# Pair slots of a vision tower on one core: values' products in another bank, the rank a slot later, the second norm's scale behind the transposes

## The chip, the cores and the metric

The kernel runs on one core of one Trainium2 chip. The metric is the device time of one execution in microseconds (us). The engines named below are TensorE (PE in the rows, its weight loads PEld), VectorE (DVE), ScalarE (ACT), GpSimd (POOL) and SyncE (SP, which issues DMAs). The engines run their own instruction streams in order and meet only at semaphores.

## The reference

Three stages follow each other: a patch tokenizer, windowed attention at several pooling levels, and a transformer block with a mixture of experts. The change lies in the third:

```python
def _L0_ffn_ref(x, norm1_w, norm1_b, qkv_w, ...):
    xn = _layernorm(x, norm1_w, norm1_b)                    # 64 images, 49 tokens, 192 features, 12 heads
    qkv = (xn @ qkv_w.T + qkv_b).reshape(Bx, Nx, 3, H, hd).transpose(2, 0, 3, 1, 4)
    attn = softmax(einsum('bhqd,bhkd->bhqk', q, k) * scale)
    o = einsum('bhqk,bhkd->bqhd', attn, v)
    x = x + (o @ proj_w.T + proj_b)
    xn2 = _layernorm(x, norm2_w, norm2_b)                   # the second norm
    logits = xn2 @ w_gate                                   # 8 experts, the best 2 of each token
    gates = softmax(top_vals)
    moe_out = sum over experts of gate * (gelu(xn2 @ W1 + b1) @ W2 + b2)
    return x + moe_out
```

## The kernel before, in words

The tokenizer and the windowed attention take the first 490 us and are not touched. Then come 39 **pair slots** (490 to 840 us). Two images make a pair (`NP` = 32 pairs, 98 tokens on 128 partitions). `run_slots` runs one function per engine, `slot(item)`, and `item(lag)` is the pair that entered `lag` slots ago, so each slot works on eight pairs at different steps, n0 (just entered) to n7. Slots 0 to 7 fill the pipeline, slots 8 to 31 are full (a hardware loop of two slots a turn), slots 32 to 38 empty it. Slots 7 to 31 have all of n0 to n7.

What each engine does in a full slot is the order in which its `slot` is written out:

- GpSimd (`gpsimd`, from L499): for n0 the **root chain**, six small steps with a drain between them (L507 to L517), which turn VectorE's variance into the two scale factors of the first norm; for n4 a multiply of the normalised row by the second norm's weight (L520); for n7 a small copy of row numbers (L525) and two indirect DMAs (L529, the **scatters** of the pair's tokens to their experts' rows); for n4 the add of the second norm's bias (L532); for n3 three small steps (L536, L538, L540), which make the second norm's scale and shift, and the sum of the two residuals (L542).
- VectorE (`vector`, slot from L607): copy of the gate logits (L617), first norm's statistics (L619, L633, which releases the root chain), the maximum and subtraction for the softmax (L624, L629), the top two experts (L626 to L638), the keys spread over the heads (L644), then a wait for the root chain and the normalised row (L648), the residual (L654), the second norm's statistics, the softmax's division (L669, L673), and for n6 the **rank** of each token within its expert (L678 to L684), which is the address of the scatter that GpSimd issues in the next slot.
- ScalarE (`scalar`, slot from L779): evictions, the softmax's Exp, scaled copies. The copy of the second norm's row into the scatter's source (L820) waits until an earlier scatter has landed.
- TensorE (`tensor`, slot from L872): scores, transposes, products, in a fixed order.

After the slots VectorE counts the tokens of each expert (L690 to L730), and 56 **expert tiles** (`NT`, 128 rows each) follow, 857 to 1120 us. For a tile TensorE runs twelve products with the first weights (six on 128 rows, L967, and six on 64 rows, L970; the trace shows two passes for each product), transposes the rows of the next tile (L975, L976), and runs the second products of the tile before (L983, six of 192 columns). ScalarE applies Gelu to six blocks (L844) and then evicts the next tile's transposed rows as `xsT` (L834), for which the next tile's L967 waits.

## Time and profile before

| | us |
|---|---|
| median of 3 runs | 1167.65 (1163.40 to 1168.23) |
| the profiled execution | 1160.92 |
| its span in the trace | 1159.1 |
| pair slots in it | 490 to 843 |
| expert tiles in it | 856 to 1121 |

Busy shares over the whole span are TensorE 86%, VectorE 54%, GpSimd 48% and ScalarE 40%. They mix stages with different limits, so the stages are read one by one below. A row of the timeline gives the start in us from the span's start, the duration of the group, the engine, the line of the kernel, what it writes and reads, and in brackets how long the engine was idle before it and what ended that. "Issue" is idle time in which the engine waited for nothing that the profile shows, a drain for instance.

### The profile page before, as it was taken

The numbers are of one execution on the slowest core, as the hardware profiler recorded it, in microseconds if no ns is written. First come the engines' busy times: TensorE is split into PE (matmuls) and PEld (weight loads), VectorE is DVE, ScalarE is ACT, GpSimd is POOL, SyncE is SP. The second block draws the span as 40 slices with busy tenths as digits, with TensorE's granted clock in tenths as the row PEclk, the third lists the DMA queues.
The fourth block names the chain that finished last, engine by engine and source line by source line (L and its number), as shares of the span: only waits on it lengthen the run. The fifth ranks groups of instructions, "written<-read, shape, count | busy, mean of one in ns | idle before, by whom it ended". The sixth has DMA issues, their size and how long they took to land.

```text
span 1159.1 us, 24071 instructions
## 1 busy us (share of the span) xinstructions
PE 1000.6 (86%) x6992; PEld 856.7 (74%) x6993; DVE 630.9 (54%) x1649; ACT 467.0 (40%) x1172; POOL 561.1 (48%) x1094
## 2 busy tenths in 40 slices
PE   6969999999997898589898888988539999999960
PEld 4868898898895565377777777767429999999960
DVE  5466577475455878656766676667322222222216
ACT  1133334233204444534555555556214444444424
POOL 1385578577431223324666666666603434433430
PEclk9988999999998899799989898999559999999985
DMA  9347543562100500113500000000011111111118
GB/s 355 154 177 325 223 189 152 220 249 90 42 8 22 105 1 1 41 18 138 228 17 16 16 16 16 16 16 16 26 47 35 44 43 41 37 44 41 44 35 256
DMA packets 41701, 103.09 MB, mean 89 GB/s; under 512 B 7046, under 2 KB 28656, under 8 KB 38837
## 3 DMA queue, kind: packets, MB, share of 16 engines
q1 hardware_dynamic: 30085, 88.86, 22.1%
q0 software_dynamic: 5760, 9.68, 2.5%
q10 hardware_dynamic: 5808, 3.96, 1.1%
q8 instruction: 24, 0.39, 0.1%
q14 instruction: 24, 0.20, 0.1%
HBM read 86.30 MB, written 18.32 MB: 90 GB/s over the span
## 4 chain that ended last, share of the span: by engine, by line
PE 33%; POOLq 22%; issue 20%; DVE 9%; POOL 7%; DMA 4%; ACT 2%; DVEq 2%; SPq 1%; ACTq 0%
PE pe L1617 16%; POOLq L561 6%; POOLq L537 4%; PE pe L1626 4%; POOLq L526 2%; DMA x<-yy_d 2%; POOL xn L532 1%; POOLq L539 1%; POOLq L510 1%; POOLq L551 1%; POOL xs_d L529 1%; DVE sc L316 1%; PE pe L183 1%; PE pe L184 1%; POOLq L508 1%
## 5 line engine op out<-in xcount | busy, mean ns | idle before, releaser
L1617 PE MATMUL pe<-wm,xm 128*128 128x193 f32 x1008 | 176.6, 335 | 2.2 <-DVEq L1421 2.2
L1617 PEld LDWEIGHTS pe<-wm,xm 128*128 128x128 f32 x1008 | 170.8, 195 | 6.6 <-issue 4.0
L844 ACT ACTIVATE hT<-pe,eb 128x128 f32<-128x128 f32 x336 | 93.0, 376 | 147.4 <-PE pe L970 147.4
L983 PE MATMUL pp<-w2s,hT 128*128 x672 | 118.5, 326 | 0.0
L983 PEld LDWEIGHTS pp<-w2s,hT 128*128 128x128 f32 x672 | 107.9, 190 | 0.2
L967 PE MATMUL pe<-xsT,ew 128*128 128x128 f32 x672 | 90.3, 286 | 3.5 <-ACT xsT L834 3.5
L967 PEld LDWEIGHTS pe<-xsT,ew 128*128 128x128 f32 x672 | 81.6, 196 | 9.1 <-ACT xsT L834 4.1
L529 POOL DMA_INDIRECT xs_d<-xsrc,dst x64 | 65.5, 1023 | 40.5 <-issue 40.5
L759 DVE TENSOR_TENSOR ys<-pp,b2s 128x192 f32<-128x192 f32 x56 | 20.0, 358 | 117.2 <-PE pp L983 117.2
L557 POOL DMA_INDIRECT yy_d<-ys,yix x56 | 57.2, 1021 | 46.5 <-issue 46.5
L1346 POOL TENSOR_TENSOR sqs<-sqs,sqt 128x448 f32<-128x448 f32 x56 | 67.3, 1202 | 8.0 <-issue 0.2
L563 POOL TENSOR_TENSOR xdum<-xdum 128x1 f32<-128x1 f32 x56 | 21.3, 381 | 101.6 <-issue 86.1
L898 PE MATMUL pp<-xT,wqk 128*96 128x128 f32 x512 | 66.7, 287 | 0.9 <-issue 0.9
L898 PEld LDWEIGHTS pp<-xT,wqk 128*96 128x96 f32 x512 | 63.8, 177 | 1.7 <-issue 1.6
L1247 ACT ACTIVATE sqt<-xm 128x2688 f32<-128x2688 f32 x14 | 34.3, 2447 | 73.0 <-POOL sqs L1346 50.1
L751 DVE COPY eb<-b1s 128x6 f32 x56 | 9.6, 171 | 87.5 <-issue 73.2
L644 DVE TENSOR_TENSOR kbd<-pp,const 96x294 f32<-96x294 f32 x128 | 50.2, 451 | 8.4 <-PE pp L898 8.3
L1626 PE MATMUL pe<-ww,wv 128*128 128x193 f32 x300 | 53.5, 327 | 0.0
L183 PE MATMUL pe<-wqkv,stg 96*128 96x288 f32 x128 | 44.8, 432 | 9.7 <-ACT stg L228 7.0
L970 PE MATMUL pe<-xsT,ew 64*128 64x128 f32 x672 | 53.1, 291 | 0.0
L1626 PEld LDWEIGHTS pe<-ww,wv 128*128 128x128 f32 x300 | 49.7, 189 | 0.6 <-DVEq L1447 0.6
L160 POOL TENSOR_TENSOR ob<-pv 128x576 f32<-128x576 f32 x11 | 15.4, 1402 | 71.2 <-PE pt L202 63.4
(267 smaller groups left out, 2242.1 us busy)
## 6 DMA issues: line engine op xcount, KB each, us to landing
xm<-in_xm SPq DMA_DIRECT2D x7, 2688.0 KB, 15.7
raw<-in_xwa SPq DMA_DIRECT2D x7, 1792.0 KB, 7.6
raw<-in_xwb SPq DMA_DIRECT2D x7, 1536.0 KB, 10.9
x<-in_x SPq DMA_DIRECT2D x4, 1536.0 KB, 8.9
xs<-xs_d SPq DMA_DIRECT2D x56, 96.5 KB, 1.9
x<-yy_d SPq DMA_DIRECT2D x8, 672.0 KB
w1s<-in_W SPq DMA_DIRECT2D x1, 4608.0 KB, 15.4
w2s<-in_W SPq DMA_DIRECT2D x1, 4608.0 KB, 25.4
```

Source lines behind the costliest of these rows:

```text
L183: mm(y[:, n, 0:288], stg[0:H2, u, 0, s], self.wqkv[0:H2, 0, n * 288:(n + 1) * 288], start=True, stop=False)
L529: g.indirect_dma_start(self.xs_d[:, :], bass.IndirectOffsetOnAxis(ap=self.dst[:, u, k:k + 1], axis=0), self.xsrc[:, u, k], None, bounds_ch ...
L557: g.indirect_dma_start(self.yy_d[:, :], bass.IndirectOffsetOnAxis(ap=self.yix[:, u:u + 1], axis=0), self.ys[:, u], None, bounds_check=2 * ...
L561: pool.drain()
L844: last = f(self.hT[:, u, c], pe1[:, 2 * u + c % 2, (c // 2) * ROWS:(c // 2 + 1) * ROWS], ACT.Gelu, bias=self.b1[:, u, c:c + 1])
L898: last = mm(pp[0:H2, g, m * P:(m + 1) * P], self.wqk[:, h, g * D + m * H2:g * D + (m + 1) * H2], self.xT2[:, h], start=(h == 0), stop=(h = ...
L967: mm(chunk(n), self.w1[:, u, n * P:(n + 1) * P], self.xsT[:, n % 2], start=(n < 2), stop=False, skip_group_check=True)
L970: last = mm(chunk(n), self.w1[r, u, HID + (n // 2) * P:HID + (n // 2 + 1) * P], self.xsT[r, 1 - n % 2], start=False, stop=True, skip_group ...
L983: last = mm(pp[:, u, 0:D], self.hT[:, u, n], self.w2s[:, bass.ds(e, 1), n * D:(n + 1) * D].rearrange("p o d -> p (o d)"), start=(n == 0), ...
L1346: last = nc.gpsimd.tensor_tensor(dst, dst, src[c], ALU.add)
L1617: mm(y[:, 0:D + 1], cell(q, c), wm[:, q, c], start=(q + c == 0), stop=(q == 3 and c == KC - 1))
L1626: mm(y[:, 256:256 + D + 1], wave(wv, wv6, q), ww[:, q], start=(q == 0), stop=(q == 5))
```

## The change

Line numbers behind an arrow are those of the changed kernel.

- **The rank a slot later.** VectorE's rank steps leave the end of n6's slot and stand in the next slot, right behind the normalised row that waits for the root chain. GpSimd's scatter for n7 still is in that same slot.
- **The second norm's weight and bias** are no longer applied to rows by GpSimd (L520 and L532 are gone). ScalarE applies them as scale and bias of the evictions behind the transposes: of the gate's transposes in the slot (L797), and of `xsT` in the expert tiles (L834, now two instructions of 128 columns in place of one of 256). The scale and shift of a row are kept for every pair in a new tile `rn`, which GpSimd fills with one more small copy (L537 after), and the scatter's source is made by ScalarE straight from the residual one slot later.
- **GpSimd** has one drain more, at the end of its slot.
- **The statistics of the first norm** come at the front of VectorE's slot, ahead of the softmax's maximum.
- **The attention's products with the values** go to the bank of the keys (`pp[..., 1, 256:]`) and no longer to the scores' bank; TensorE's order in the slot changes: scores, rank, the second norm's transposes, queries and keys, the attention output's transposes, values, gate logits, the softmax's transposes, projection, attention times values, the first norm's transposes. Its passes of few columns (rank, gate logits, attention times values) stand apart now. The projection stands behind the softmax's transposes, and the products for keys wait for the division (L673) of the slot before.
- The tile `n2` shrinks to two columns for each half, and its two loads become one.

The diff, without the semaphores' names, the load of `n2` and TensorE's order:

```diff
@@ -515,21 +516,15 @@
                 g.tensor_tensor(st[:, 3:4], st[:, 3:4], eps, ALU.add)
                 pool.drain()
                 g.tensor_tensor(st[:, 3:4], st[:, 3:4], mhalf, ALU.pow).then_inc(self.a_r, 1)
-            if b:
-                pool.wait_ge(self.c_x, b[0] + 1)
-                g.tensor_tensor(self.xn[:, b[1]], self.xn[:, b[1]], self.n2[:, 0], ALU.mult)
             if d:
                 i, u, _ = d
-                pool.wait_ge(self.d_src, i + 2)
+                pool.wait_ge(self.d_src, i + 1)
                 pool.wait_ge(self.d_dst, i + 1)
                 g.tensor_copy(self.xsrc[:, u, :, D:DX], self.const[:, C_ROW:C_ROW + 2 * NP].rearrange("p (i k) -> p i k", k=2)[:, bass.ds(i, 1), :].rearrange("p o k -> p k o"))
-            pool.drain()
-            if d:
+                pool.drain()
                 for k in range(2):
                     g.indirect_dma_start(self.xs_d[:, :], bass.IndirectOffsetOnAxis(ap=self.dst[:, u, k:k + 1], axis=0),
                                          self.xsrc[:, u, k], None, bounds_check=E * R - 1, oob_is_err=False).then_inc(self.scat[u], 16)
-            if b:
-                g.tensor_tensor(self.xn[:, b[1]], self.xn[:, b[1]], self.n2[:, 1], ALU.add).then_inc(self.c_xn, 1)
             if c:
                 i = c[0]
                 pool.wait_ge(self.c_var, i + 1)
@@ -537,9 +532,12 @@
                 pool.drain()
                 g.tensor_tensor(st[:, 8:9], st[:, 8:9], mhalf, ALU.pow)
                 pool.drain()
-                g.tensor_scalar(st[:, 9:10], st[:, 6:7], st[:, 8:9], -1.0, ALU.mult, ALU.mult).then_inc(self.c_r, 1)
+                g.tensor_scalar(st[:, 9:10], st[:, 6:7], st[:, 8:9], -1.0, ALU.mult, ALU.mult)
+                pool.drain()
+                g.tensor_copy(self.rn[:, bass.ds(i, 1), :].rearrange("p o k -> p (o k)"), st[:, 8:10]).then_inc(self.c_r, 1)
                 rows = [t[:, bass.ds(i, 1), :].rearrange("p o d -> p (o d)") for t in (self.hall, self.x2)]
                 g.tensor_tensor(rows[0], rows[0], rows[1], ALU.add).then_inc(self.res_set, 1)
+            pool.drain()
         run_slots(pool, NP, 8, slot)
 
...
@@ -606,18 +603,20 @@
 
         def slot(item):
 
-            n0, n1, n2, n3, n6 = (item(lag) and item(lag)[0] for lag in (0, 1, 2, 3, 6))
+            n0, n1, n2, n3, n6, n7 = (item(lag) and item(lag)[0] for lag in (0, 1, 2, 3, 6, 7))
             lg = self.lg
             dve.drain()
+            if n0 is not None:
+                v.bn_stats(self.bn[:, 0], row(hall, n0))
             if n6 is not None:
                 m8 = self.m8[:, item(6)[1]]
                 if not isinstance(n6, int) or n6 > 1:
                     dve.wait_ge(self.d_eg, n6 - 1)
                 dve.wait_ge(self.d_lg, n6 + 1)
                 v.tensor_copy(lg[:], pe1[:, 3, 256:256 + E]).then_inc(self.d_lgo, 1)
+            dve.drain()
             if n0 is not None:
-                v.bn_stats(self.bn[:, 0], row(hall, n0))
-            dve.drain()
+                v.bn_aggr(st[:, 0:2], self.bn[:, 0]).then_inc(self.a_var, 1)
             if n2 is not None:
                 dve.wait_ge(self.b_s, n2 + 1)
                 sc = pe1[:, 0:2, 0:6 * T].rearrange("p n (h k) -> p n h k", h=6)
@@ -629,8 +628,6 @@
                 v.tensor_tensor(self.pm[:].rearrange("p (n h) k -> p n h k", n=2)[:, :, :, 0:T], sc,
                                 self.mx2[:].rearrange("p (n h) -> p n h", n=2).unsqueeze(3).to_broadcast([P, 2, 6, T]),
                                 ALU.subtract).then_inc(self.b_sub, 1)
-            if n0 is not None:
-                v.bn_aggr(st[:, 0:2], self.bn[:, 0]).then_inc(self.a_var, 1)
             if n6 is not None:
                 v.max_index(self.i8[:], m8, lg[:])
             dve.drain()
@@ -648,40 +645,40 @@
                 v.tensor_scalar(row(x2, n0), row(hall, n0), st[:, 0:1], st[:, 2:3], ALU.subtract, ALU.mult).then_inc(self.a_x, 1)
                 if isinstance(n0, int) and n0 < 5:
                     self.mixed(dve, [3 * n0 + 1, 3 * n0 + 2] if n0 else [2, 3])
+            if n7 is not None:
+                u, h = item(7)[1:]
+                dve.wait_ge(self.d_rank, n7 + 1)
+                t = self.t8
+                v.tensor_tensor(t[:, 1:3], self.oh[:], self.pt1[:, 1:2, 0:E].to_broadcast([P, 2, E]), ALU.mult)
+                v.tensor_tensor(self.acc[:], self.acc[:], self.ohs[:], ALU.add)
+            dve.drain()
+            if n7 is not None:
+                v.tensor_reduce(self.df[:], t[:, 1:3], X, ALU.add)
+            if n6 is not None:
+                v.tensor_tensor(self.oh[:], const[:, C_EI:C_EI + E].unsqueeze(1).to_broadcast([P, 2, E]),
+                                self.idx[:].unsqueeze(2).to_broadcast([P, 2, E]), ALU.is_equal)
+            dve.drain()
+            if n7 is not None:
+                dve.wait_ge(self.scat[u], 32 * h)
+                v.tensor_scalar(self.dst[:, u], self.df[:], const[:, C_VAL + 1:C_VAL + 2], None, ALU.add).then_inc(self.d_dst, 1)
+            if n6 is not None:
+                v.tensor_tensor(self.ohs[:], self.oh[:, 0], self.oh[:, 1], ALU.add).then_inc(self.d_oh, 1)
             if n3 is not None:
                 dve.wait_ge(self.c_r, n3)
                 dve.wait_ge(self.c_proj, n3 + 1)
                 v.tensor_tensor(row(x2, n3), row(x2, n3), pe1[:, 2, 256:256 + D], ALU.add)
-            dve.drain()
-            if n6 is not None:
-                v.tensor_tensor(self.oh[:], const[:, C_EI:C_EI + E].unsqueeze(1).to_broadcast([P, 2, E]),
-                                self.idx[:].unsqueeze(2).to_broadcast([P, 2, E]), ALU.is_equal)
-            if n3 is not None:
+                dve.drain()
                 v.bn_stats(self.bn[:, 1], row(x2, n3))
-            dve.drain()
-            if n6 is not None:
-                v.tensor_tensor(self.ohs[:], self.oh[:, 0], self.oh[:, 1], ALU.add).then_inc(self.d_oh, 1)
-            if n3 is not None:
+                dve.drain()
                 v.bn_aggr(st[:, 6:8], self.bn[:, 1]).then_inc(self.c_var, 1)
-            o = pe1[:, 0, 0:AH * (AHD + 1)].rearrange("p (h d) -> p h d", h=AH)
+            o = pp[:, 1, 256:256 + AH * (AHD + 1)].rearrange("p (h d) -> p h d", h=AH)
             if n2 is not None:
                 dve.wait_ge(self.b_pv, n2 + 1)
                 v.reciprocal(self.mx2[:], o[:, :, AHD:AHD + 1].rearrange("p h o -> p (h o)"))
-            dve.drain()
-            if n2 is not None:
+                dve.drain()
                 dve.wait_ge(self.c_T, n2)
                 v.tensor_tensor(self.on[:].rearrange("p (h d) -> p h d", h=AH), o[:, :, 0:AHD],
                                 self.mx2[:].unsqueeze(2).to_broadcast([P, AH, AHD]), ALU.mult).then_inc(self.b_on, 1)
-            if n6 is not None:
-                dve.wait_ge(self.d_rank, n6 + 1)
-                t = self.t8
-                v.tensor_tensor(t[:, 1:3], self.oh[:], self.pt1[:, 1:2, 0:E].to_broadcast([P, 2, E]), ALU.mult)
-                v.tensor_tensor(self.acc[:], self.acc[:], self.ohs[:], ALU.add)
-                dve.drain()
-                v.tensor_reduce(self.df[:], t[:, 1:3], X, ALU.add)
-                dve.drain()
-                dve.wait_ge(self.scat[item(6)[1]], 32 * item(6)[2])
-                v.tensor_scalar(self.dst[:, item(6)[1]], self.df[:], const[:, C_VAL + 1:C_VAL + 2], None, ALU.add).then_inc(self.d_dst, 1)
             if isinstance(n0, int) and 0 < n0 < 5:
                 self.mixed(dve, [3 * n0 + 3])
...
+            if n5 is not None:
+                act.wait_ge(self.c_nT, n5 + 1)
+                for h in range(2):
+                    last = f(self.xnT2[0:H2, h], pe1[0:H2, 3, h * P:(h + 1) * P], ACT.Identity, bias=colg[:, h, 6:7], scale=colg[:, h, 5:6])
+                last.then_inc(self.d_out, 1)
...
@@ -802,6 +802,10 @@
             if n0 is not None:
                 act.wait_ge(self.a_x, n0 + 1)
                 f(self.xh2[:], self.x2[:, bass.ds(n0, 1), :].rearrange("p o d -> p (o d)"), ACT.Copy, scale=self.st[:, 3:4]).then_inc(self.a_xh, 1)
+            if n4 is not None:
+                act.wait_ge(self.c_r, n4 + 1)
+                f(self.xn[:, item(4)[1]], row(self.x2, n4), ACT.Identity, bias=col(n4, 1), scale=col(n4, 0)).then_inc(self.c_x, 1)
+            if n0 is not None:
                 act.wait_ge(self.a_T, n0 + 1)
                 for h in range(2):
                     last = f(self.xT2[0:H2, h], pt1[0:H2, 0, h * P:(h + 1) * P], ACT.Identity, bias=colg[:, h, 4:5], scale=colg[:, h, 3:4])
@@ -813,15 +817,13 @@
                         src = pp[m * B:m * B + T, 0, 256:256 + D].rearrange("p (h e d) -> p h e d", e=2, d=AHD)[:, :, e]
                         last = f(self.vbd[e * B:e * B + T, m, :, e * (AHD + 1):e * (AHD + 1) + AHD], src, ACT.Copy)
                 last.then_inc(self.a_v, 1)
-            if n5 is not None:
-                u = item(5)[1]
-                act.wait_ge(self.c_xn, n5 + 1)
-                act.wait_ge(self.scat[u], 32 * item(5)[2])
-                f(self.xsrc[:, u, :, 0:D], self.xn[:, u:u + 1].to_broadcast([P, 2, D]), ACT.Copy).then_inc(self.d_src, 1)
             if n6 is not None:
+                u = item(6)[1]
                 act.wait_ge(self.d_oh, n6 + 1)
-                m8 = self.m8[:, item(6)[1]]
+                m8 = self.m8[:, u]
                 f(self.egs[:, bass.ds(n6, 1)], m8[:, 0:1], ACT.Exp, bias=m8[:, 1:2], scale=-1.0).then_inc(self.d_eg, 1)
+                act.wait_ge(self.scat[u], 32 * item(6)[2])
+                f(self.xsrc[:, u, :, 0:D], self.x2[:, bass.ds(n6, 1), :].to_broadcast([P, 2, D]), ACT.Identity, bias=col(n6, 1), scale=col(n6, 0)).then_inc(self.d_src, 1)
         run_slots(act, NP, 8, slot)
         act.wait_ge(self.meta_set, 1)
         self.zero_tails(act, range(1, E, 2))
@@ -831,7 +833,9 @@
                 return
             i, u, h = b
             act.wait_ge(self.e_T, i + 3)
-            f(self.xsT[:], pt1[:, u, 0:2 * ROWS].rearrange("p (h n) -> p h n", h=2), ACT.Copy).then_inc(self.e_xT, 1)
+            for h in range(2):
+                last = f(self.xsT[:, h], pt1[:, u, h * ROWS:(h + 1) * ROWS], ACT.Identity, bias=self.n2[:, h, 1:2], scale=self.n2[:, h, 0:1])
+            last.then_inc(self.e_xT, 1)
 
         def hidden(item):
...
```

How it stands in the instruction streams. GpSimd, one full slot of the loop before, from the root chain's last step; `xn` is the second norm's row, `xs_d` the experts' rows in memory:

```order
L517 TENSOR_TENSOR st<-st,const 128x1
L520 TENSOR_TENSOR xn<-xn,n 128x192 [waits c_x]
L524 REGISTER_ALU [waits d_src]
L525 ISA [waits d_dst]
L525 COPY xsrc<-const 128x2
L529 DMA xs_d<-xsrc,dst 26240x193 x2
L532 TENSOR_TENSOR xn<-xn,n 128x192
L536 TENSOR_TENSOR st<-st,const 128x1 [waits c_var]
L538 TENSOR_TENSOR st<-st,const 128x1
L540 TENSOR_SCALAR st<-st 128x1
L542 TENSOR_TENSOR hall<-hall,x 128x192
```

And the changed kernel at the same place:

```order
L518 TENSOR_TENSOR st<-st,const 128x1
L523 ISA [waits d_dst,d_src]
L523 COPY xsrc<-const 128x2
L526 DMA xs_d<-xsrc,dst 26240x193 x2
L531 TENSOR_TENSOR st<-st,const 128x1 [waits c_var]
L533 TENSOR_TENSOR st<-st,const 128x1
L535 TENSOR_SCALAR st<-st 128x1
L537 COPY rn<-st 128x2
L539 TENSOR_TENSOR hall<-hall,x 128x192
```

The multiply and the add on `xn` are gone, the copy `rn` is new, and the wait for the rank's address (`d_dst`) stands right behind the root chain.

VectorE, one full slot of the loop before, from the row that waits for the root chain (`a_r`); `dst` is the scatter's address:

```order
L648 TENSOR_SCALAR x<-hall,st 128x192 [waits a_r]
L654 TENSOR_TENSOR x<-x,pe 128x192 [waits c_proj,c_r]
L657 TENSOR_TENSOR oh<-const,idx 128x16
L660 BN_STATS bn<-x 128x6
L663 TENSOR_TENSOR ohs<-oh 128x8
L665 BN_AGGR st<-bn 128x2
L669 RECIPROCAL mx<-pe 128x12 [waits b_pv]
L673 TENSOR_TENSOR on<-pe,mx 128x192 [waits c_T]
L678 TENSOR_TENSOR t<-oh,pt 128x16 [waits d_rank]
L679 TENSOR_TENSOR acc<-acc,ohs 128x8
L681 TENSOR_REDUCE df<-t 128x2
L684 TENSOR_SCALAR dst<-df,const 128x2 [waits scat1]
```

And the changed kernel at the same place:

```order
L645 TENSOR_SCALAR x<-hall,st 128x192 [waits a_r]
L652 TENSOR_TENSOR t<-oh,pt 128x16 [waits d_rank]
L653 TENSOR_TENSOR acc<-acc,ohs 128x8
L656 TENSOR_REDUCE df<-t 128x2
L658 TENSOR_TENSOR oh<-const,idx 128x16
L663 TENSOR_SCALAR dst<-df,const 128x2 [waits scat0]
L665 TENSOR_TENSOR ohs<-oh 128x8
L669 TENSOR_TENSOR x<-x,pe 128x192 [waits c_proj,c_r]
L671 BN_STATS bn<-x 128x6
L673 BN_AGGR st<-bn 128x2
L677 RECIPROCAL mx<-pp 128x12 [waits b_pv]
L680 TENSOR_TENSOR on<-pp,mx 128x192 [waits c_T]
```

The address `dst`, which GpSimd waits for, was made at the slot's end for the next slot's scatter; now it is made between the normalised row and the residual for the scatter of the same slot.

ScalarE in the expert tiles, two tiles of the stage's start before; `hT` is the Gelu's output, `xsT` the next tile's rows:

```order
L844 ACTIVATE hT<-pe,eb 128x128 [waits e_wc]
L844 ACTIVATE hT<-pe,eb 128x128 x5
L834 ACTIVATE xsT<-pt 128x256 [waits e_T]
L844 ACTIVATE hT<-pe,eb 128x128 [waits e_h,y_free,e_wc]
L844 ACTIVATE hT<-pe,eb 128x128 x5
L834 ACTIVATE xsT<-pt 128x256 [waits e_T]
```

And the changed kernel at the same place:

```order
L848 ACTIVATE hT<-pe,eb 128x128 [waits e_wc]
L848 ACTIVATE hT<-pe,eb 128x128 x5
L837 ACTIVATE xsT<-pt,n 128x128 [waits e_T]
L837 ACTIVATE xsT<-pt,n 128x128
L848 ACTIVATE hT<-pe,eb 128x128 [waits e_h,y_free,e_wc]
L848 ACTIVATE hT<-pe,eb 128x128 x5
L837 ACTIVATE xsT<-pt,n 128x128 [waits e_T]
L837 ACTIVATE xsT<-pt,n 128x128
```

Each tile's eviction of `xsT`, behind the six Gelus, has become two instructions.

## Rows read from the trace of the kernel before

**Rows 1.** The page's slices: TensorE's busy tenths and its granted clock, 29 us each.
```profile
PE   6969999999997898589898888988539999999960
...
PEclk9988999999998899799989898999559999999985
```

**Rows 2.** The chain of work that ended last, 690 to 710 us, by line.
```profile
by line: issue 30.4%; POOLq L537 19.0%; POOLq L526 11.5%; POOL xn L532 6.0%; POOLq L539 5.9%; POOLq L510 5.8%; POOLq L508 4.8%; POOL xs_d L529 3.9%; POOL xsrc L525 2.4%; POOLq L512 2.2%; POOLq L514 2.2%; POOLq L516 2.2%; POOL st L536 1.4%; 
```

**Rows 3.** Timeline of one pair slot, GpSimd: start us, us, engine, line, op [idle before].
```profile
699.25 0.59 POOL L520 TENSOR_TENSOR xn<-xn,n 128x192 f32<-128x192 f32 x1
...
699.78 0.21 POOL L525 COPY xsrc<-const 128x2 f32 x1
...
700.87 1.08 POOL L529 DMA_INDIRECT xs_d<-xsrc,dst  x1 [0.87 <-issue]
...
702.26 0.97 POOL L529 DMA_INDIRECT xs_d<-xsrc,dst  x1 [0.30 <-issue]
...
703.24 0.60 POOL L532 TENSOR_TENSOR xn<-xn,n 128x192 f32<-128x192 f32 x1
...
704.78 0.57 POOL L538 TENSOR_TENSOR st<-st,const 128x1 f32<-128x1 f32 x1 [0.79 <-issue]
...
705.61 0.26 POOL L540 TENSOR_SCALAR st<-st 128x1 f32<-128x1 f32 x1 [0.26 <-issue]
...
705.83 0.59 POOL L542 TENSOR_TENSOR hall<-hall,x  x1
...
706.38 0.18 POOL L507 TENSOR_TENSOR st<-st,const 128x1 f32<-128x1 f32 x1
```

**Rows 4.** Timeline, GpSimd: the root chain's first step in slots 6, 7 and 31.
```profile
551.44 0.19 POOL L507 TENSOR_TENSOR st<-st,const 128x1 f32<-128x1 f32 x1 [2.95 <-DVE st L633]
...
560.09 0.19 POOL L507 TENSOR_TENSOR st<-st,const 128x1 f32<-128x1 f32 x1 [1.99 <-DVE st L633]
...
793.46 0.19 POOL L507 TENSOR_TENSOR st<-st,const 128x1 f32<-128x1 f32 x1
```

**Rows 5.** Timeline, VectorE after the root chain in that slot; the rank's steps, tail.
```profile
699.40 0.55 DVE L648 TENSOR_SCALAR x<-hall,st  x1 [1.95 <-POOL st L517]
...
699.87 0.34 DVE L654 TENSOR_TENSOR x<-x,pe 128x192 f32 x1
...
834.43 0.17 DVE L678 TENSOR_TENSOR t<-oh,pt 128x16 f32<-128x16 f32 x1 [3.34 <-PE pt L950]
...
835.00 0.23 DVE L684 TENSOR_SCALAR dst<-df,const 128x2 int32<-128x2 f32 x1
835.36 0.19 POOL L525 COPY xsrc<-const 128x2 f32<-128x2 f32 x1 [0.76 <-DVE dst L684]
```

**Rows 6.** Timeline, GpSimd: the step in a slot without scatters; the last slot's scatter.
```profile
537.29 0.55 POOL L538 TENSOR_TENSOR st<-st,const 128x1 f32<-128x1 f32 x1
...
841.49 0.98 POOL L529 DMA_INDIRECT xs_d<-xsrc,dst  x1 [2.06 <-issue]
```

**Rows 7.** Timeline of one expert tile: TensorE, its weight loads (PEld) and ScalarE.
```profile
937.81 1.93 PEld L983 LDWEIGHTS pp<-w2s,hT 128*128 128x128 f32 x12
...
939.36 0.42 ACT L834 ACTIVATE xsT<-pt 128x256 f32<-128x256 f32 x1
939.82 1.41 PEld L967 LDWEIGHTS pe<-xsT,ew 128*128 128x128 f32 x12
...
941.36 0.94 PE L970 MATMUL pe<-xsT,ew 64*128 64x128 f32 x12
...
942.43 1.66 ACT L844 ACTIVATE hT<-pe,eb 128x128 f32<-128x128 f32 x6 [2.65 <-PE pe L970]
```

**Rows 8.** Timeline, ScalarE: the load of Gelu's table, and an Identity pair after it.
```profile
466.57 1.28 ACT L238 ACT_TABLE_LOAD   x1
...
498.02 0.80 ACT L807 ACTIVATE xT<-pt,colg 96x128 f32<-96x128 f32 x2 [0.52 <-PE pt L943]
```

**Rows 9.** Timeline, TensorE near the end of the pair slots: it waits for GpSimd.
```profile
830.74 0.66 PE L917 MATMUL pe<-const,xn 128*96 128x128 f32 x2 [2.50 <-POOL xn L532]
```

109 lines of the change are left out of this document (54 added, 55 removed).

## The prediction

> **What bounds the kernel now.** I read the page's slices first. TensorE is busy 8 to 9 tenths through most of the span, and its granted clock is near full except for two slices near 840 us [rows 1]. So TensorE could be the bound everywhere, and the share alone doesn't tell. Next I read the chain of waits in the pair slots. From 690 to 710 us it runs through GpSimd and its queue alone: every share in the row is a GpSimd step, a drain of its queue or issue [rows 2]. So in a full slot GpSimd's own instruction stream is the bound. The timeline of one slot shows that stream without a hole that another engine would end: all its idle times are "issue", that is, drains and the preparation of the scatters [rows 3]. VectorE is the one that waits: 1.95 us for the root chain's last step in the slot shown [rows 5]. The root chain starts at 560.09 us in slot 7 and at 793.46 in slot 31 [rows 4]: 233.4 us over 24 slots, 9.72 us each. Before slot 7 there are no scatters, GpSimd waits 2 to 3 us for VectorE's variance, and the interval from slot 6 to slot 7 is 8.65 us [rows 4].
>
> In the expert tiles two chains close at the same time. The last weight load of L983 ends at 939.74, ScalarE's eviction of `xsT` ends at 939.78, and the next tile's first load begins at 939.82 [rows 7]. Hence TensorE is never seen idle, yet the eviction has no slack. The loop is: L970 ends (942.30), Gelu begins (942.43), `xsT` begins 1.5 us later, takes 0.42, then L967 and L970 of the next tile. A tile takes 4.59 us (939.82 to the next tile's load, by the Gelu that follows).
>
> **The change part by part.**
>
> *Rank behind the root chain.* GpSimd now waits for `dst` of n7 in the slot in which it scatters it. VectorE makes `dst` behind the normalised row, and the normalised row waits for GpSimd's root chain. So GpSimd finishes the root chain, and then stands still while VectorE does the row and the rank. Queued behind that wait on GpSimd are the copy, both scatters, the second norm's small steps, the residual sum and the next root chain, that is, the whole bound stream. Its length from the start of the row: 0.47 us until VectorE's next instruction can start (699.40 to 699.87); 0.80 from the rank's first step to the end of `dst` (834.43 to 835.23); one small step `oh` that now stands between, at most its 0.17, taken as 0.10; 0.13 from `dst` to GpSimd's copy (835.23 to 835.36) [rows 5]. That is 1.50 us. Before, the copy began 0.38 us after that row (699.78 against 699.40) [rows 3, 5], since only the multiply stood there. The copy is 1.12 us later in each slot. The multiply's 0.59 is already in this term: it goes, and the wait takes its place and more. The wait for `xsrc` (`d_src`) was satisfied before and has a whole slot now, so it costs nothing.
>
> *The bias add (L532).* It takes 0.60 us on GpSimd, but it stands behind the second scatter, which ends at 703.23. The step L538 starts 1.55 us later with 0.79 us of idle before it; in a slot without scatters the same step shows no idle time [rows 3, 6]. In the last slot, where a scatter follows a scatter with only the copy between, 2.06 us pass idle before it, against 0.87 in a full slot [rows 3, 6]. So the first drain behind a scatter ends about 1.5 us after it, whatever stands between. The add is hidden in it, and its removal gives nothing. If I am wrong it gives up to 0.55 us a slot. I take 0, because the last slot's row shows the delay with no add at all.
>
> *The copy into `rn` and the last drain.* A drain between small steps costs 0.17 to 0.26 us, the small copy 0.21 (as L525), and the residual sum started 0.22 after L540 [rows 3]. With drain and copy between it starts about 0.60 after it: +0.38 (0.35 to 0.47). The new drain at the end makes the next root chain start 0.59 + 0.17 after the sum's start, where it was 0.55: +0.21 (to 0.30).
>
> *A full slot* so grows by 1.12 + 0.38 + 0.21 = 1.71 us, from 9.72 to 11.4. Over 24 intervals that is 41 us, and slot 31's own wait adds 1.1: **+42 us** (from +28 with the add given back to +48).
>
> *Other engines in the slot.* VectorE, ScalarE and TensorE have 2 us of slack against GpSimd before and more in the longer slot; the new places of projection, values and evictions lie under it, and so does the second instruction for the gate's eviction. Should GpSimd cease to be the bound they would matter; the 8.65 us of slot 6 is what they take together without scatters.
>
> *Filling and emptying.* The variance is released ahead of the softmax's maximum, so GpSimd's 2 to 3 us of waiting in slots 6 and 7 [rows 4] should shrink; slots 1 to 4 are filled by TensorE's mixing products. I take -3 us (0 to -8). In the last slots TensorE waited 2.50 us for GpSimd's bias add behind two scatters [rows 9]; this wait goes, and with it the multiply in slots 32 to 35. But the scatters of the last slots keep their own spacing. I take -3 us (0 to -5).
>
> *Expert tiles.* `xsT` becomes two instructions with scale and bias from columns. The nearest row is such a pair for 96 partitions, 0.80 us together [rows 8], against 0.42 for the single copy [rows 7]: +0.38 us. The lower bound is two steps of the Gelu group, 1.66/6 = 0.28 each [rows 7], so +0.13. With no slack this goes into each of 55 intervals: **+21 us** (+7 to +21). The Trainium skill ("ScalarE: Activation LUTs", section "What ACT_TABLE_LOAD costs") states 186 ns + 0.833 ns for each column of an instruction, about 93 ns more for each pointer operand, and an overlap of about 93 ns between two instructions; an estimate by it is 0.86 us for the pair and 0.40 for the copy, so the tiles would give +25. For the copy the trace agrees, with 0.42. A table change between Gelu and Identity would be far dearer, but an Identity pair runs at 498.02 after Gelu's table was loaded at 466.57, with only a wait for TensorE before it [rows 8], so none is expected.
>
> Sum against the profiled execution: 1160.9 + 42 + 21 - 3 - 3 = 1218 us. Its time is 6.7 us under the median of the runs, 1167.65, so the median is forecast at **1224 us**.
>
> **The rivals.**
>
> *A, the drain behind the scatter shrinks.* Without the add, L538 follows as in a slot without scatters: -0.55 and -0.64 of the 0.79. A slot grows by 0.52 us only, 24 of them by 12.5, and the sum is 1167.65 + 12.5 + 1.1 + 21 - 6 = 1196 us. Against it speaks the last slot's row.
>
> *B, TensorE's clock falls and TensorE becomes the bound.* In the slices near 840 us TensorE is busy 5 and 3 tenths and its clock is half (1.2 GHz); in the full slots it is busy over 8 tenths and mostly at 2.4 GHz [rows 1]. The same work in 11.4 us would be about 7 tenths, between the two. At half clock 8 us of passes would become up to 16; if a quarter of the slots ran so and took 14 us, that is 6 x 2.6 = 16 us more: 1240 us. The Trainium skill ("TensorE: Matmul & The Clock Gate", section "What's actually happening") says that the throttled state is the default and activity releases it, which speaks for this rival; the trace agrees in kind, and the price above is from the rows.
>
> *C, the pair for `xsT` costs its lower bound.* Then the tiles give 7 instead of 21: 1210 us.
>
> *D, the other side: GpSimd ceases to be the bound.* If the adds and multiplies on rows were what held its stream, and `dst` were ready when GpSimd asks, the slot would fall to the 8.65 us of slot 6: 24 x (8.65 - 9.72) = -26, with the tiles' +21 and the edges' -6 gives 1157 us. It decides at a GpSimd stream under 8.65 us a slot. Against it: 3.45 us from copy to the end of the scatters and 1.55 behind them stay, and the wait for `dst` can't begin before the root chain ends.
>
> **How the numbers follow.** My forecast, 1214 to 1234, has 0.60; A 0.12; B 0.12; C 0.10; D 0.06. The range from 1198 to 1244 takes in C, most of B, and the unknown costs of the drains, and leaves out D and about half of A. Beyond 0.5% (6 us, about what a measurement of this kernel can tell from no change) slower is everything but D: 0.93; within it 0.02; faster 0.05.
>
> **What would show it.** In the changed trace the root chain's first step should repeat every 11.4 us; GpSimd's copy (L523) should show an idle time of about 1.6 us ended by VectorE's `dst` (L663); the small power step (L533) should still start 1.5 us after the second scatter. The expert tile should take 4.97 us, with TensorE waiting 0.3 to 0.4 us for `xsT` (L837). If the copy doesn't wait, D or an error in my order of events holds; if L533 follows at once, A; if a tile stays at 4.6 us, the eviction had slack after all; if the clock in the slots is near 0.7, B.

## The result, and the profile of the changed kernel

The changed kernel takes 1235.71 us (median of 4 runs, 1234.11 to 1237.96), the kernel before 1167.38 us beside it. The ratio is 1.0593 with a 95% interval of 1.0568 to 1.0618: slower by 5.9%. The forecast was 1224 us with a range of 1198 to 1244, and 1214 to 1234 as its likeliest part.

The profiled execution took 1235.71 us, its span is 1233.9 us. By stages, from the starts of the root chain's first step (slots 0, 7 and 31) and of the first and the last instruction of L967 (L974 after the change), all in us. The last one stands 1.3 us into the last tile, so the tiles' stretch is 55 tile lengths and 1.3 us:

| stretch | before | after | difference | forecast |
|---|---|---|---|---|
| start to root chain of slot 0 | 493.97 | 494.66 | +0.7 | 0 |
| slot 0 to slot 7 (filling) | 66.12 | 61.80 | -4.3 | -3 |
| slot 7 to slot 31 (24 intervals) | 233.37 | 286.06 | +52.7 | +41 |
| slot 31 to first tile | 63.9 | 63.1 | -0.8 | -2 |
| first to last tile (55 intervals) | 258.2 | 286.0 | +27.8 | +21 |
| last tile to end | 43.6 | 42.3 | -1.3 | 0 |
| span | 1159.1 | 1233.9 | +74.8 | +57 |

The page's slices of the changed kernel, to be laid beside [rows 1]: TensorE's busy tenths and its granted clock, 31 us each.

```profile
PE   7969999999987985898887888887359999999970
...
PEclk9979999999988997998788888889569999999995
```

In the full pair slots (the 21st to the 27th slice) the granted clock is mostly a step lower than before. TensorE waits more: it is busy for 191 of the 234 us from 608 to 842 us (82%), where it was busy for 172 of 193 us (89%), and its granted clock averages 0.84 there, where it was 0.94. That TensorE does not set the pace there is seen in GpSimd's stream. One slot of it, the timeline from 725 to 737 us, which answers to [rows 3] (start, duration, engine, line, operation, and the idle time before it with what ended it):

```profile
725.35 0.19 POOL L508 TENSOR_TENSOR st<-st,const 128x1 f32<-128x1 f32 x1 [0.23 <-issue]
...
727.38 0.55 POOL L518 TENSOR_TENSOR st<-st,const 128x1 f32<-128x1 f32 x1
729.56 0.19 POOL L523 COPY xsrc<-const 128x2 f32 x1 [1.62 <-DVE dst L663]
730.62 1.09 POOL L526 DMA_INDIRECT xs_d<-xsrc,dst  x1 [0.88 <-issue]
732.02 0.97 POOL L526 DMA_INDIRECT xs_d<-xsrc,dst  x1 [0.30 <-issue]
733.01 0.21 POOL L531 TENSOR_TENSOR st<-st,const 128x1 f32<-128x1 f32 x1
734.70 0.57 POOL L533 TENSOR_TENSOR st<-st,const 128x1 f32<-128x1 f32 x1 [1.48 <-issue]
...
735.92 0.19 POOL L537 COPY rn<-st 128x2 f32 x1 [0.23 <-issue]
736.08 0.59 POOL L539 TENSOR_TENSOR hall<-hall,x  x1
737.32 0.19 POOL L508 TENSOR_TENSOR st<-st,const 128x1 f32<-128x1 f32 x1 [0.65 <-issue]
```

The copy L523 is released by VectorE's `dst`, 4.21 us after the root chain's start, where it followed at 3.07 us before. L533 starts 1.71 us after the second scatter's end and 1.57 in the next slot (1.55 in [rows 3]), although the bias add is gone. At the end stand the new copy with its drain and 0.65 us before the next root chain, where there was no idle time. In the next interval, which doesn't close GpSimd's loop, that last wait is 0.24 and the slot is 11.48 us long, against 11.97 for this one.

VectorE in the next slot (timeline, 740 us), which answers to [rows 5]: the normalised row, the rank's first step, and `dst` behind it.

```profile
740.03 0.38 DVE L645 TENSOR_SCALAR x<-hall,st  x1 [4.47 <-POOL st L518]
740.33 0.16 DVE L652 TENSOR_TENSOR t<-oh,pt 128x16 f32<-128x16 f32 x1
...
741.06 0.23 DVE L663 TENSOR_SCALAR dst<-df,const 128x2 int32<-128x2 f32 x1 [0.17 <-issue]
```

VectorE had been idle for 4.47 us when the root chain released it, and did the rank only then. GpSimd waited for `dst` 23 times between 560 and 830 us, 37.6 us in all; the forecast for one wait was 1.6.

One expert tile (timelines of the weight loads, of TensorE and of ScalarE), which answers to [rows 7]:

```profile
1001.51 1.41 PEld L974 LDWEIGHTS pe<-xsT,ew 128*128 128x128 f32 x12 [0.52 <-ACT xsT L837]
```

```profile
1001.51 1.60 PE L974 MATMUL pe<-xsT,ew 128*128 128x128 f32 x12 [0.22 <-ACT xsT L837]
1003.04 0.94 PE L977 MATMUL pe<-xsT,ew 64*128 64x128 f32 x12
...
1006.53 0.71 PE L974 MATMUL pe<-xsT,ew 128*128 128x128 f32 x4 [0.23 <-ACT xsT L837]
```

```profile
1004.11 1.67 ACT L848 ACTIVATE hT<-pe,eb 128x128 f32<-128x128 f32 x6 [2.66 <-PE pe L977]
1005.63 0.84 ACT L837 ACTIVATE xsT<-pt,n 128x128 f32<-128x128 f32 x2
```

The eviction takes 0.84 us for 0.42, TensorE now waits for it, and the tile is 5.02 us long for 4.59.

### The profile page after: what moved, and what is told of

Same layout as the page of the kernel before. It is cut to its first block, busy times and chain, and to the rows that moved or that the text cites. A ratio compares the mean times of both kernels' runs of the same rounds, so it can differ in the third digit from the quotient of the medians.

```text
span 1233.9 us, 24280 instructions
## 1 busy us (share of the span) xinstructions
PE 1034.4 (84%) x6992; PEld 880.0 (71%) x6993; DVE 623.9 (51%) x1649; ACT 517.6 (42%) x1260; POOL 534.0 (43%) x1062
## 3 DMA queue, kind: packets, MB, share of 16 engines
q0 software_dynamic: 5760, 9.68, 2.3%
## 4 chain that ended last, share of the span: by engine, by line
PE 42%; POOLq 14%; issue 13%; ACT 11%; DVE 10%; POOL 4%; DMA 3%; DVEq 2%; SPq 1%; ACTq 0%
PE pe L1623 14%; PE pe L974 7%; ACT hT L848 6%; POOLq L532 4%; PE pe L977 4%; PE pe L1632 3%; ACT xsT L837 3%; POOLq L540 1%; DMA x<-yy_d 1%; POOLq L534 1%; POOL xs_d L526 1%; POOLq L511 1%; DVE sc L316 1%; POOL st L518 1%; PE pe L183 1%
## 5 line engine op out<-in xcount | busy, mean ns | idle before, releaser
L974 PE MATMUL pe<-xsT,ew 128*128 128x128 f32 x672 | 92.4, 289 | 19.3 <-ACT xsT L837 19.3
L974 PEld LDWEIGHTS pe<-xsT,ew 128*128 128x128 f32 x672 | 81.7, 196 | 35.6 <-ACT xsT L837 35.6
L911 PE MATMUL pp<-xT,wqk 128*96 128x128 f32 x512 | 89.3, 349 | 1.2 <-issue 0.9
L911 PEld LDWEIGHTS pp<-xT,wqk 128*96 128x96 f32 x512 | 85.1, 225 | 4.0 <-issue 3.3
L555 POOL DMA_INDIRECT yy_d<-ys,yix x56 | 60.2, 1074 | 46.7 <-issue 46.7
L837 ACT ACTIVATE xsT<-pt,n 128x128 f32<-128x128 f32 x112 | 47.2, 496 | 17.7 <-PE pt L983 17.7
L956 PE MATMUL pt<-const,xh 128*96 128x128 f32 x64 | 13.8, 298 | 48.0 <-ACT xh L804 48.0
L561 POOL TENSOR_TENSOR xdum<-xdum 128x1 f32<-128x1 f32 x56 | 11.3, 201 | 98.8 <-issue 87.3
L645 DVE TENSOR_SCALAR x<-hall,st (+1 forms) x32 | 12.1, 377 | 76.4 <-POOL st L518 76.4
```

Source lines behind the costliest of these rows:

```text
L555: g.indirect_dma_start(self.yy_d[:, :], bass.IndirectOffsetOnAxis(ap=self.yix[:, u:u + 1], axis=0), self.ys[:, u], None, bounds_check=2 * ...
L837: last = f(self.xsT[:, h], pt1[:, u, h * ROWS:(h + 1) * ROWS], ACT.Identity, bias=self.n2[:, h, 1:2], scale=self.n2[:, h, 0:1])
L911: last = mm(pp[0:H2, g, m * P:(m + 1) * P], self.wqk[:, h, g * D + m * H2:g * D + (m + 1) * H2], self.xT2[:, h], start=(h == 0), stop=(h = ...
L974: mm(chunk(n), self.w1[:, u, n * P:(n + 1) * P], self.xsT[:, n % 2], start=(n < 2), stop=False, skip_group_check=True)
```

## The experiments

Ratios are to the kernel before in the same set of runs, with 95% intervals; times are medians. Experiments 1 to 4 put the two large terms to the test, each from both sides; 5 to 8 the drain behind a scatter; 9 the small steps; 10 to 12 look for a faster kernel. The kernels of experiments 1 and 5 leave out a part of the second norm (its weight and bias for the experts, and its bias), so they measure time only. "Slot" is the mean interval between root chains from slot 11 to slot 31: 9.68 us before, 11.73 after.

**1. `tile_one_copy`: the tiles' eviction as one copy, in the changed kernel.**

```
-            for h in range(2):
-                last = f(self.xsT[:, h], pt1[:, u, h * ROWS:(h + 1) * ROWS], ACT.Identity, bias=..., scale=...)
-            last.then_inc(self.e_xT, 1)
+            f(self.xsT[:], pt1[:, u, 0:2 * ROWS].rearrange(...), ACT.Copy).then_inc(self.e_xT, 1)
```

> The changed kernel with the expert tiles' xsT evicted by one ScalarE copy, as before; norm-2's weight and bias are left out for the experts' input. Theory 1 (xsT has no slack in a tile): the copy takes 0.42 us in place of 0.84, a steady tile goes from 5.02 back to 4.59, the stretch from the first to the last gate-weight matmul of the tiles from 286 to some 258 us, and the time from 1235.7 to 1208 to 1212. Rival (the tiles got longer by TensorE's clock or by their neighbours' timing): the tile stays at 4.9 or above and the time within 5 us of 1235.7. The pair slots stay at 11.5 to 12.0 us under both.

Measured: 1209.0 us, ratio 1.0337 (1.0280 to 1.0394). The tiles' stretch is 258.7 us (906.9 to 1165.6), the slot stays at 11.72. Theory 1 holds: the pair of instructions costs 27 us.

**2. `tile_two_in_before`: the pair of instructions alone, in the kernel before.**

```
-            f(self.xsT[:], pt1[:, u, 0:2 * ROWS].rearrange(...), ACT.Copy).then_inc(self.e_xT, 1)
+            for h in range(2):
+                last = f(self.xsT[:, h], pt1[:, u, h * ROWS:(h + 1) * ROWS], ACT.Identity, bias=self.n2[:, 1, 0:1], scale=self.n2[:, 0, 0:1])
+            last.then_inc(self.e_xT, 1)
```

> The kernel before with xsT evicted by two ScalarE instructions (scale and bias from one column of the norm-2 weight and bias, so these are applied a second time) and nothing else changed. Theory 1 (the pair of instructions alone makes the longer tile): tile 4.59 to 5.0, time 1167.4 plus 21 (my forecast for this term) to 28 (what the tiles' stretch grew by), so 1188 to 1195. Rival (part of the tiles' growth came from the pair stage, as a different phase of the DMA queues or of the clock at their start): plus 21 or less, with tiles at 4.59 in part of the stretch. The pair stage stays as it was.

Measured: 1197.3 us beside 1170.7, ratio 1.0241 (1.0187 to 1.0294), so +26.6 us. The tiles' stretch is 286.9 us for 258.2; the slot is 9.71. The pair brings the whole growth with it. Part of it lies beyond 5.02 us a tile: apart from the stretch's first two, 17 of the 55 intervals are 5.14 to 5.50 us long here, and 7 are 5.18 to 5.57 us long in the changed kernel. The kernel before has none (4.59 us in nearly all), but neither have experiments 6, 7 and 9, which carry the same pair. So the long tiles are not a fixed cost of it.

What such a long tile looks like, from the changed kernel's timelines of TensorE and ScalarE:

```profile
1145.65 0.94 PE L977 MATMUL pe<-xsT,ew 64*128 64x128 f32 x12
...
1149.66 1.60 PE L974 MATMUL pe<-xsT,ew 128*128 128x128 f32 x12 [0.74 <-ACT xsT L837]
```

```profile
1147.24 1.66 ACT L848 ACTIVATE hT<-pe,eb 128x128 f32<-128x128 f32 x6 [3.18 <-PE pe L977]
```

Gelu starts 0.65 us after the end of the matmuls that it needs, where it is 0.13 us in the tile at 1004 us; the eviction behind it is late by as much. TensorE's clock is full there. What holds ScalarE back was not settled.

**3. `rank_before_x`: the rank's arithmetic ahead of the row, in the changed kernel.**

```
+            if n7 is not None:
+                ...
+                dve.wait_ge(self.d_rank, n7 + 1)
+                ... (product, acc, sum, dst, moved here)
             if n0 is not None:
                 dve.wait_ge(self.a_r, n0 + 1)
```

> The changed kernel with VectorE's rank arithmetic of item n7 (product, acc, sum, dst) put ahead of x, in the 2 to 4.5 us in which VectorE waits for GpSimd's root, rather than behind it. Theory 1 (the copy into xsrc waits for dst alone): the gap between the root chain's end and the copy falls from 1.6 us to 0.3 to 0.5, the slot from 11.72 to some 10.6, 24 slots and the emptying ones give 25 to 30 us: 1206 to 1211. Rival (the scatter's landing or the drain behind it sets the slot, so an earlier copy only waits longer later): the drain behind the scatters grows by what the copy gains, and the time stays within 8 us of 1235.7.

Measured: 1199.0 us, ratio 1.0244 (1.0188 to 1.0300): 36.7 us less than the changed kernel, more than the 25 to 30 expected. Its GpSimd timeline shows the copy right behind the root chain, and an unchanged drain behind the scatters:

```profile
606.19 0.19 POOL L508 TENSOR_TENSOR st<-st,const 128x1 f32<-128x1 f32 x1 [0.24 <-issue]
...
608.72 0.19 POOL L523 COPY xsrc<-const 128x2 f32 x1
...
611.17 0.97 POOL L526 DMA_INDIRECT xs_d<-xsrc,dst  x1 [0.30 <-issue]
...
613.88 0.57 POOL L533 TENSOR_TENSOR st<-st,const 128x1 f32<-128x1 f32 x1 [1.52 <-issue]
```

The copy is at 2.53 us after the slot's start: 1.68 earlier than in the changed kernel, and 0.54 earlier than in the kernel before, because norm 2's multiply no longer stands between. My expectation had forgotten that the wait hid this gain too. The slot is 10.18 us. In four of the 24 intervals (slots 7, 9, 15 and 23) the copy still waited 1.24 to 1.69 us for `dst`, and these are 11.6 to 14.6 us long (slot 7, the longest, with a drain of 4.58 us beside the load); the other 20 have a mean of 10.0 us. In all four VectorE's `kbd`, which stands ahead of the rank, had waited for TensorE. Slot 15:

```profile
647.61 1.57 DVE L641 TENSOR_TENSOR kbd<-pp,const 96x294 f32<-96x294 f32 x4 [2.41 <-PE pp L911]
...
```

**4. `rank_after_x_in_before`: the same move the other way, alone, in the kernel before.**

```
-            if n6 is not None:
-                dve.wait_ge(self.d_rank, n6 + 1)
-                ... (product, acc, sum, dst, at the slot's end)
+            if n7 is not None:
+                dve.wait_ge(self.d_rank, n7 + 1)
+                ... (the same, behind x)
             if n3 is not None:
                 dve.wait_ge(self.c_r, n3)
```

> The kernel before with VectorE's rank arithmetic moved from the end of one slot to behind x of the next, and nothing else changed. Theory 1 (my forecast's first term): GpSimd's copy starts 4.2 us after its root chain in place of 3.07, the slot goes from 9.68 to 10.8, 24 slots and the emptying ones add 27 to 30 us: ratio 1.023 to 1.026. Rival (undoing it in the changed kernel gave 37 us since it also brought scores, gates or a clock forward): plus 33 or more here if that holds both ways, and under 20 if the new order of TensorE is what makes the rank late.

Measured: 1189.4 us beside 1162.1, ratio 1.0236 (1.0205 to 1.0267), so +27.3 us. The copy stands 1.10 us idle until `dst`, 4.23 us after the slot's start; the slot is 10.83, +1.15:

```profile
702.12 0.18 POOL L507 TENSOR_TENSOR st<-st,const 128x1 f32<-128x1 f32 x1
...
706.35 0.18 POOL L525 COPY xsrc<-const 128x2 f32 x1 [1.10 <-DVE dst L660]
```

This is the forecast's first term (+1.12 a slot, 27 us) by itself, with TensorE's order untouched.

**5. `before_no_add`: without the bias add behind the scatters, in the kernel before.**

```
-                g.tensor_tensor(self.xn[:, b[1]], self.xn[:, b[1]], self.n2[:, 0], ALU.mult)
+                g.tensor_tensor(self.xn[:, b[1]], self.xn[:, b[1]], self.n2[:, 0], ALU.mult).then_inc(self.c_xn, 1)
...
-                g.tensor_tensor(self.xn[:, b[1]], self.xn[:, b[1]], self.n2[:, 1], ALU.add).then_inc(self.c_xn, 1)
```

> The kernel before without GpSimd's add of norm-2's bias behind the scatters (L532; the bias is left out) and nothing else changed. Theory 1 (mine in the prediction: the first drain behind a scatter ends at a fixed time after it, whatever stands between): from the second scatter's end to L538 the same 1.5 to 1.6 us, the idle time before L538 grows from 0.8 to 1.3 us, the slot stays at 9.68 and the time within 4 us of before. Rival A (the drain only waits for the work ahead of it): the slot falls by the add's own length, some 0.5 us, the 24 full slots give 12 us, so 1155 for 1167.

Measured: 1160.7 us beside 1164.3, ratio 0.9967 (0.9952 to 0.9983). The slot is 9.63 for 9.68. GpSimd's timeline:

```profile
703.13 0.97 POOL L529 DMA_INDIRECT xs_d<-xsrc,dst  x1 [0.30 <-issue]
...
705.67 0.57 POOL L536 TENSOR_TENSOR st<-st,const 128x1 f32<-128x1 f32 x1 [1.35 <-issue]
```

From the second scatter's end to the second norm's root it is 1.57 us, 1.55 with the add [rows 3]; the idle time took the add's place, 1.35 for 0.79. Rival A falls. Of the 3.7 us gained, the slots from 11 on show 1.1, and slots 7 to 11 took 1.2 more than before; the rest isn't seen in the profiled spans, 1158.6 and 1159.1 us.

**6. `hall_behind_scatter`: 0.6 us of other work moved into that gap, in the changed kernel.**

```
                 pool.wait_ge(self.c_var, i + 1)
+                rows = [t[:, bass.ds(i, 1), :].rearrange("p o d -> p (o d)") for t in (self.hall, self.x2)]
+                g.tensor_tensor(rows[0], rows[0], rows[1], ALU.add).then_inc(self.res_set, 1)
                 g.tensor_tensor(st[:, 8:9], st[:, 7:8], eps, ALU.add)
...
-                rows = [...]
-                g.tensor_tensor(rows[0], rows[0], rows[1], ALU.add).then_inc(self.res_set, 1)
```

> The changed kernel with GpSimd's add of x2 onto hall (0.59 us) put directly behind the second scatter, ahead of the second norm's first operation, rather than at the slot's end. Theory 1 (work placed between a scatter and the first drain behind it costs nothing, since that drain ends 1.7 to 1.9 us after the scatter anyway): the idle time before L533's operation falls from 1.4 to some 0.8 us, the slot falls by 0.55 to 0.6 us, 24 slots and the emptying ones give 14 to 16 us: 1220 to 1222. Rival (the drain lasts 1.4 us from its own start): the slot stays at 11.7 and the time within 4 us of 1235.7.

Measured: 1215.6 us, ratio 1.0438 (1.0402 to 1.0474), 20 us less than the changed kernel. The slot is 11.11 (-0.62), the idle time before L535 is 0.8 to 0.9 and the root starts 1.55 to 1.7 us after the scatter's end. 15 us come from the 24 slots as expected, 2 from the emptying slots and 4 from the tiles' stretch, 281.8 us here, which has no long tiles.

**7. `cover_filled`: the gap filled beyond its end.** As 6, and

```
+                for k in range(2):
+                    g.tensor_tensor(self.fill[:, k], self.const[:, 0:D], self.const[:, 0:D], ALU.add)
                 g.tensor_tensor(st[:, 8:9], st[:, 7:8], eps, ALU.add)
```

> As hall_behind_scatter, with two more GpSimd operations of the add's size (0.55 us each, constants into a spare tile) behind the add onto hall, so that 1.85 us of work stands between the second scatter and the first drain behind it. Theory 1 (the drain ends when its own work is done or 1.6 us after the scatter, whichever is later): the second norm's root starts 2.0 us after the scatter's end in place of 1.6, the slot grows from 11.10 by 0.4 and the ratio is 1.052 (that of hall_behind_scatter 1.044). Rival (a drain behind a scatter costs 0.8 us whatever stands ahead of it): slot plus 1.1, ratio 1.066.

Measured: 1224.2 us, ratio 1.0544 (1.0507 to 1.0582); slot 11.52, +0.41 on experiment 6.

```profile
704.58 0.97 POOL L527 DMA_INDIRECT xs_d<-xsrc,dst  x1 [0.30 <-issue]
705.56 0.60 POOL L533 TENSOR_TENSOR hall<-hall,x  x1
706.11 0.97 POOL L535 TENSOR_TENSOR fill<-const 128x192 f32<-128x192 f32 x2
...
707.54 0.57 POOL L538 TENSOR_TENSOR st<-st,const 128x1 f32<-128x1 f32 x1 [0.32 <-issue]
```

With 1.7 us of work in the gap the idle time falls to 0.32 and the root starts 1.99 us after the scatter. So the drain has an end that is fixed by the scatter, at 1.55 to 1.7 us, and work ahead of it is free up to about 1.3 us. That figure is an estimate, the 1.7 us of work less the 0.4 us that it cost; no run put just that much in the gap.

**8. `load_later`: the experts' weights loaded later, in the changed kernel.**

```
         sp.wait_ge(self.mix_mm, NP // 2)
+        sp.wait_ge(self.scat[0], 32 * 4)
```

> The changed kernel with the loads of the experts' weights (10 MB) held back until the first eight pairs have been scattered, so that they run beside slots 15 to 17 or so rather than up to slot 8. Theory 1 (the first drain behind the scatters lasts until they land, and they land late behind the loads' packets): slots 7 to 9 have drains of 1.3 to 1.5 us (now 4.25, 2.88, 1.84) and the long ones move to the slots beside the loads; the time changes by less than 5 us. Rival A (the first scatters are slow in themselves): slots 7 to 9 keep their 4.25, 2.88 and 1.84 and nothing shows beside the loads. Rival B (TensorE's idle time and lower clock in slots 8 and 9 make them long): the same drains, but slots at 11.7 once the clock is back.

Measured: 1238.3 us, ratio 1.0582 (1.0526 to 1.0639). First slot 7 of the changed kernel, where the load ends at about 567 us. Then slots 7 and 14 of this one, the second of them beside the load that now runs from 639 to 666 us:

```profile
563.37 0.98 POOL L526 DMA_INDIRECT xs_d<-xsrc,dst  x1 [0.30 <-issue]
...
568.83 0.57 POOL L533 TENSOR_TENSOR st<-st,const 128x1 f32<-128x1 f32 x1 [4.25 <-issue]
```

```profile
568.71 0.57 POOL L533 TENSOR_TENSOR st<-st,const 128x1 f32<-128x1 f32 x1 [1.35 <-issue]
...
654.37 0.57 POOL L533 TENSOR_TENSOR st<-st,const 128x1 f32<-128x1 f32 x1 [5.06 <-issue]
```

The idle times of slots 7 to 9 were 4.25, 2.88 and 1.84 us and are now 1.35, 1.39 and 1.64; slots 14 and 15, both of which now scatter beside the load, went from 1.33 and 1.56 to 5.06 and 3.48. The long drains go with the load. This costs and gives back the same, so the time doesn't change.

**9. `rn_direct`: without the copy into `rn`, its drain and the drain at the slot's end, in the changed kernel.**

```
                 g.tensor_tensor(st[:, 8:9], st[:, 7:8], eps, ALU.add)
+                g.tensor_scalar(st[:, 9:10], st[:, 6:7], -1.0, None, ALU.mult)
...
-                g.tensor_tensor(st[:, 8:9], st[:, 8:9], mhalf, ALU.pow)
+                g.tensor_tensor(rn[0], st[:, 8:9], mhalf, ALU.pow)
                 pool.drain()
-                g.tensor_scalar(st[:, 9:10], st[:, 6:7], st[:, 8:9], -1.0, ALU.mult, ALU.mult)
-                pool.drain()
-                g.tensor_copy(self.rn[:, bass.ds(i, 1), :].rearrange("p o k -> p (o k)"), st[:, 8:10]).then_inc(self.c_r, 1)
+                g.tensor_tensor(rn[1], st[:, 9:10], rn[0], ALU.mult).then_inc(self.c_r, 1)
...
-            pool.drain()
```

> The changed kernel with the second norm's root and product written to rn by the operations that make them (the mean's sign is turned by an operation of its own beside the first add, in the cover of the drain behind the scatters), without the copy, without the drain ahead of it and without the drain at the slot's end. Theory 1 (these are on GpSimd's path in full): copy 0.19 and its drain 0.23 go, and the end of the slot gives back 0.27 and, at the loop's end, 0.69; the slot falls from 11.70 to 10.8 to 11.1, 24 slots give 14 to 20 us: 1215 to 1221. Rival (the root's chain waits for something else at the slot's start, as dst did in the middle): under 6 us.

Measured: 1208.6 us, ratio 1.0388 (1.0353 to 1.0422), 27 us less than the changed kernel. The gain is more than the 14 to 20 us expected. The slot is 10.80 (-0.93), where 10.8 was the best that I expected; slots 7 to 11 (-3.2), the emptying slots (-2) and the tiles' stretch (281.9, -4) give what is beyond. The intervals no longer alternate: 10.77 and 10.81 us.

**10. `before_hall`: the add onto `hall` in the gap, in the kernel before.** The edit is that of experiment 6.

> The kernel before with the add of x2 onto hall (0.59 us) put directly behind the scatters and norm 2's bias add, ahead of the second norm's first operation. Theory 1 (up to some 1.5 us of work behind a scatter is free, for the first drain ends 1.55 us after it): the idle time before the second norm's root falls from 0.8 to 0.25 us, slot 9.68 to 9.1 or 9.2, 24 slots 12 to 15 us: ratio 0.987 to 0.990. Rival (the drain lasts at least 0.8 us from its own start): ratio 1.00.

Measured: 1154.0 us, ratio 0.9937 (0.9916 to 0.9958). Less than expected: the slot is 9.33, -0.36 and not -0.55. GpSimd's timeline:

```profile
701.26 0.57 POOL L540 TENSOR_TENSOR st<-st,const 128x1 f32<-128x1 f32 x1 [0.42 <-issue]
702.00 0.27 POOL L542 TENSOR_SCALAR st<-st 128x1 f32<-128x1 f32 x1 [0.17 <-issue]
702.51 0.19 POOL L507 TENSOR_TENSOR st<-st,const 128x1 f32<-128x1 f32 x1 [0.25 <-issue]
```

The add had itself covered something at its old place: the next slot's first step, which followed it at once [rows 3], now comes 0.25 us after a shorter one. This holds for one interval of two, those in which GpSimd's loop of two slots closes. In the slot ahead of the one shown the step follows at once:

```profile
693.01 0.19 POOL L507 TENSOR_TENSOR st<-st,const 128x1 f32<-128x1 f32 x1
```

The intervals alternate between 9.14 us, which is the whole of the expected gain, and 9.50.

**11. `before_mended`: as 10, with the eviction on VectorE.**

```
                 dve.drain().then_inc(self.e_wc, 1)
+                dve.wait_ge(self.e_T, i + 3)
+                dve.wait_ge(self.e_h, i)
+                v.tensor_copy(self.xsT[:], self.pt1[:, u, 0:2 * ROWS].rearrange("p (h n) -> p h n", h=2)).then_inc(self.e_xT, 1)
...
-            f(self.xsT[:], pt1[:, u, 0:2 * ROWS].rearrange(...), ACT.Copy).then_inc(self.e_xT, 1)
```

> As before_hall, and the experts' xsT evicted by one VectorE copy behind the copy of the expert's weights in place of ScalarE's. It shows how far the kernel before comes with the two cheap edits of all_mended alone: 12 to 15 us from the slots and, with a tile at 4.53 for 4.59 as in all_mended, 5 to 7 from the tiles: ratio 0.981 to 0.985, above all_mended's 0.968, if the order of the change (no product and no add of norm 2 on GpSimd) is worth 0.5 us a slot. If it is worth nothing, the ratio is 0.968 here too.

Measured: 1148.3 us, ratio 0.9883 (0.9854 to 0.9913). The ratio is above the 0.981 to 0.985 expected. The tiles' stretch is 251.5 us for 258.2, as expected; the slots give only the 9 us of experiment 10.

**12. `all_mended`: the changed kernel with all of it.** Edits 3, 6 and 9, and the eviction on VectorE with norm 2's weight and bias:

```
+                for k in range(2):
+                    last = v.tensor_scalar(self.xsT[:, k], self.pt1[:, u, k * ROWS:(k + 1) * ROWS], self.n2[:, k, 0:1], self.n2[:, k, 1:2], ALU.mult, ALU.add)
+                last.then_inc(self.e_xT, 1)
```

> The changed kernel with the rank's arithmetic ahead of x, the second norm written to rn directly, the add onto hall directly behind the scatters, no drain at the slot's end, and the experts' xsT (weight and bias of norm 2 included) evicted by two VectorE instructions behind the copy of the expert's weights in place of two of ScalarE. Theory 1 (each term is on GpSimd's path and they add up; TensorE alone bounds a tile): slot 10.0 less 0.6 less 0.6 = 8.8 to 9.0 us, against 9.68 before; tile 4.59; some 1235.7 - 67 - 27 = 1142, faster than before by 2 per cent. Rival (with GpSimd at 9.0, VectorE's wait for TensorE's qk matmuls, or TensorE itself, paces the slots at 9.5 to 10): 1155 to 1165, about the kernel before.

Measured: 1126.3 us (1125.15 to 1130.0), ratio 0.9681 (0.9644 to 0.9717): faster than the kernel before by 3.2%, and 16 us under what I expected. One slot of GpSimd, and one tile of TensorE and of VectorE:

```profile
703.81 0.19 POOL L508 TENSOR_TENSOR st<-st,const 128x1 f32<-128x1 f32 x1
...
706.34 0.18 POOL L523 COPY xsrc<-const 128x2 f32 x1
...
708.79 0.97 POOL L526 DMA_INDIRECT xs_d<-xsrc,dst  x1 [0.30 <-DVE st L672]
...
711.48 0.57 POOL L537 TENSOR_TENSOR rn<-st,const 128x1 f32 x1 [0.76 <-issue]
...
712.70 0.19 POOL L508 TENSOR_TENSOR st<-st,const 128x1 f32<-128x1 f32 x1 [0.22 <-issue]
```

```profile
954.37 1.50 PE L966 MATMUL pe<-xsT,ew 128*128 128x128 f32 x12
...
956.94 2.12 PE L982 MATMUL pp<-w2s,hT 128*128 x12
958.89 1.28 PE L966 MATMUL pe<-xsT,ew 128*128 128x128 f32 x10
```

```profile
957.35 0.73 DVE L753 TENSOR_SCALAR xsT<-pt,n 128x128 f32<-128x128 f32 x2 [0.26 <-PE pt L975]
```

The slot is 8.72 us. The single edits took 1.54, 0.93 and 0.62 off 11.73, which leaves 8.64: they add up, as steps of one serial stream do. GpSimd still sets the pace: no hole in the slot shown is ended by another engine, apart from the 0.30 between the scatters, as long as ever. The exceptions are slots 7 and 9, where the copy waited 1.71 and 2.93 us for `dst`. TensorE's clock from 599 to 773 us is 1.00. The eviction ends at 958.1 us, ahead of TensorE's need at 958.9, so a tile is 4.53 us of back to back TensorE work and the stretch 251.3 us. The rest of the 16 us: the emptying slots take 57.5 us from slot 31 to the first tile, 5.6 less than in the changed kernel, and the tiles gained 35 rather than 27.

## Why the prediction was right, and where its sum was off

**The rank's wait: right.** Forecast +1.12 us a slot, 27 us over 24. In the changed kernel the copy starts 1.14 us later in the slot, and the move alone in the kernel before costs 1.15 a slot and 27.3 us. Undone in the changed kernel it gives 37 us, not 27, since the same wait also hides the 0.54 us of the removed multiply. I had put that in the term by starting it from where the copy stood before; the two experiments are the two sides of it.

**The bias add: right, to 0.06 us a slot.** Its removal alone gives 0.06 us a slot, and the drain ends 1.57 us after the scatter with or without it. Rival A named 0.52 us for the growth of a slot; it is 2.04.

**The copy into `rn` and the last drain: the mechanism right, the size not.** Forecast 0.38 and 0.21. The add onto `hall` starts 0.65 us after the step ahead of it, where it was 0.22: 0.43. The slot's end is the mis-sized term: in one interval of two the next root chain starts 0.24 us after the end of the add (forecast), in the other 0.65. Before, the add covered both. Over the two kinds of interval the end costs about 0.48 in place of 0.21, and 1.14 + 0.43 + 0.48 make 2.05, where 2.04 was measured from slot 11 on and 1.71 forecast. Over 20 intervals this is 6.6 us. `rn_direct` gives the two terms back together, 0.93 a slot. That the 0.65 stands where GpSimd's loop closes is read from its alternation, here and in `before_hall`, and no run took the loop away.

**The first slots with scatters: not foreseen.** I took 9.72 us as every slot's length and added one growth to all. From slot 7 to 11 the changed kernel needs 11.9 us more, not 6.8. The filling is 4.3 us shorter (forecast 3), so slot 7's scatter is issued at 563.37 us beside the end of the weights' load, where it was at 565.93. `load_later` shows that the load makes these drains long; it accounts for 4.7 of the 5.1 us. The gain of the filling was given back there. Slots 8 and 9 scatter after the load's end and still have long drains, which they lose with the load; but in `rank_before_x`, with the load beside slot 7 as here, slot 8's idle time is 1.33. What was late in the changed kernel's slot 8 is the landing itself: its second scatter landed 3.86 us after its start, 2.3 to 2.5 being usual, although the DMA engines were nearly idle from 569 us on. How the load reaches into the next slots stays open.

**The expert tiles: right cause, 7 us short.** Forecast +0.38 us by the pair of 96 partitions, 55 times. The pair of 128 partitions takes 0.84, the tile grows by 0.43 (24 us), the 7 long tiles bring 3, and the stretch's first two tiles 1. Both kernels with the pair alone or without it agree: 27 us. The Trainium skill's figures ("ScalarE: Activation LUTs", section "What ACT_TABLE_LOAD costs") gave the estimate of 0.86 us for the pair and +25 us for the tiles; the trace agrees with the first to 0.02 us, and the page's price was nearer than my row of another shape. That ScalarE's eviction had no slack was right, and so was the reading that TensorE would be the one to wait.

**Emptying: 1 us short.** Slot 31 to the first tile gave 0.8 us; the forecast was -3 and +1.1 for slot 31's own wait.

**TensorE's clock (rival B).** It fell in the slots as the rival said, to 0.84, and rose to 1.00 in the fastest kernel, but it followed the slot's length and did not set it. In the changed kernel the one wait of GpSimd for another engine is that for `dst`, and VectorE's part of it was released by GpSimd's own root chain, so TensorE is not in the loop. In 19 of the 24 intervals of `rank_before_x` GpSimd waits for no engine at all. The exceptions are the four intervals of experiment 3 and 0.21 us in slot 17; in these TensorE held GpSimd back, by way of `kbd`.

**The other side (rival D).** It failed as argued: the wait for `dst` could not begin before the root chain's end. But its other half was nearly true: with `dst` ready GpSimd's stream is 8.72 us long, near the 8.65 named, and GpSimd is still the bound.

**The sum.** By the profiled executions it was 17.7 us short: 1218 for 1235.7. The 6.7 us between profile and median, which I added, did not come again, as the changed kernel's profiled execution is its median. So the forecast of the median was only 11.7 short, 6 us nearer than the stages warrant, by luck. The 1235.7 us lie inside the range, but 1.7 above the 1214 to 1234 that had the chance of 0.60, in the upper part which I had left to rival B and to the unknown costs of the drains; it was the drains, the slots beside the load and the tiles that filled it.

## What to carry to other kernels

Price a wait of the engine that is the bound from the moment at which its input can exist, not from how much idle time the producer has: VectorE had 4 us to spare and was still the cause. Look at what each instruction covers at its place before it is moved: work behind a scatter was free here up to about 1.3 us, and the same add hid 0.25 us or more at the end of every second slot. A change that fails as a whole can hold a better kernel: with the rank, the drains and the eviction put where their engines were idle, it ended 22 us under the old order with the two repairs that apply there (1126.3 and 1148.3 us, ratios 0.968 and 0.988 in their own sets).

## What the runs showed of the hardware

- The first drain on GpSimd's queue behind an indirect scatter mostly ends 1.55 to 1.8 us after the end of the scatter's row, whatever stands between, and in `cover_filled`, where the work ahead of it lasts as long as that, after 0.32 us. It ends with the landing. In slots 7 to 31 of the kernel before, the second scatter lands 2.31 to 2.83 us after its start, and the step behind the drain starts 0.21 to 0.22 us after the landing in each of the 25; in slots 7 and 8 of the changed kernel, where the landing takes 5.23 and 3.86 us, it is 0.22 and 0.21 too. The scatter at 702.26 us lands at 704.56, and the step starts at 704.78. In the changed kernel's later slots the step comes 0.21 to 0.31 us after the last landing that the trace kept, in slot 9 0.52. No run changed the landing alone. The line for all 64 scatters of the kernel before, and the DMA view from 700 to 706 us (slices of 0.15 us, busy share in tenths), in which the packets of the two scatters stand:

```profile
DMA to landing us min/median/max: 2.3/2.4/3.6
```

```profile
DMA  0000000000000000382000000931000000000000
```

- The second group of packets begins in the slice from 703.75 us, after the scatter's row has ended at 703.23 us. The Trainium skill ("Perfetto Trace Analysis", section "DMA Instruction — SWDGE (GPSIMD)") says that the profile's end of such an instruction is the end of descriptor generation and not of the transfer; the trace agrees.
- Beside a load at 371 GB/s (over 28 us, DMA share 0.96 to 0.98) the idle time before that step was 4.25 us (slot 7 of the changed kernel), 5.06 and 3.48 us (slots 14 and 15 of `load_later`), and 1.3 to 1.6 us without it. In the changed kernel's slot 8, which scatters 9 to 11 us after the load's end, it was still 2.88 us.
- With nearly the same matmuls in a slot, TensorE's granted clock over the full slots was 1.00 at 8.72 us a slot, 0.94 at 9.68 and 0.84 at 11.73.
